# Relative attention: other written-out orders for four engines, and the second head's relative products among the first head's maxima

## What is computed

```python
B, S, D, NH, DK, MRP = 2, 2048, 256, 16, 16, 64        # 32 heads in all (2 x 16)
idx = clip(r[None, :] - r[:, None], -MRP, MRP) + MRP    # distance, cut at 64
logits = einsum('bhqd,bhkd->bhqk', q, k) + einsum('bhqd,qkd->bhqk', q, embK[idx])
w = softmax(logits)
out = einsum('bhqk,bhkd->bhqd', w, v) + einsum('bhqk,qkd->bhqd', w, embV[idx])
```

## Time and profile before

| | before |
|---|---|
| median of 3 runs | 4203.42 us (4187.34 to 4205.01) |
| the profiled execution | 4198.53 us; span 4196.8 us, granted clock 0.933 |
| PE busy | 3844.2 us (92%) |
| DVE busy | 3390.2 us (81%) |
| ACT busy | 2865.1 us (68%) |
| POOL busy | 1488.6 us (35%) |
| DMA | mean 151 GB/s; SP's queue 57.9% of 16 engines' span |

### The profile page before, as it was taken

The page is one execution under the profiler, slowest core; times in us unless marked ns, Lnnn a source line. Parts: engine busy times, 40 slices in busy tenths (PEclk is TensorE's granted clock), DMA queues, the critical chain, the costliest instruction groups (busy, mean ns, idle before and its releaser), DMA issues. The chain is left out here.

```text
span 4196.8 us, 76647 instructions
## 1 busy us (share of the span) xinstructions
PE 3844.2 (92%) x26302; PEld 2105.0 (50%) x26302; DVE 3390.2 (81%) x6328; ACT 2865.1 (68%) x5771; POOL 1488.6 (35%) x1457
## 2 busy tenths in 40 slices
PE   8599999999999999996879999999999999869998
PEld 5255555555555555553533333333333333659998
DVE  7688889898998888953779999999999992657776
ACT  4077778787877777883217777777777776236666
POOL 0356667666666666651000101000001000523333
PEclk9589999999999999998969999999999996779999
DMA  8667777777777777744763424343334320789997
GB/s 313 167 144 174 163 169 177 172 177 169 172 171 169 170 168 168 168 118 135 238 124 58 72 50 77 52 72 60 63 64 70 56 60 23 172 283 325 323 326 220
DMA packets 477915, 634.98 MB, mean 151 GB/s; under 512 B 60900, under 2 KB 403668, under 8 KB 463316
## 3 DMA queue, kind: packets, MB, share of 16 engines
q1 hardware_dynamic: 458996, 606.74, 57.9%
q0 software_dynamic: 18528, 23.34, 2.9%
HBM read 412.95 MB, written 215.89 MB: 150 GB/s over the span
## 5 line engine op out<-in xcount | busy, mean ns | idle before, releaser
L1140 ACT ACTIVATE ra_p<-ra_psS 128x512 f32<-128x512 f32 x2048 | 1112.6, 602 | 328.5 <-PE ra_psS L1211 242.5
L396 DVE TENSOR_REDUCE pa_pm<-pa_psA 128x2 f32<-128x1024 f32 x1024 | 1208.6, 1220 | 136.5 <-PE pa_psA L472 136.3
L444 ACT ACTIVATE pa_p<-pa_psS 128x512 f32<-128x512 f32 x2048 | 1064.3, 603 | 297.3 <-PE pa_psS L490 293.4
L1055 DVE TENSOR_REDUCE ra_pm<-ra_psA 128x1 f32<-128x896 f32 x1024 | 1113.2, 1087 | 167.7 <-PE ra_psA L1181 110.0
L490 PE MATMUL pa_psS<-pa_qs,pa_zs 50*128 50x512 f32 x2048 | 811.3, 475 | 67.5 <-ACT pa_p L444 37.6
L1181 PE MATMUL ra_psA<-ra_zs,ra_qs 48*128 48x512 f32 x2048 | 778.0, 466 | 76.0 <-DVE ra_pm L1057 51.2
L472 PE MATMUL pa_psA<-pa_zs,pa_qs 48*128 48x512 f32 x2048 | 802.4, 475 | 33.0 <-DMA pa_zs<-k_halves 18.3
L1211 PE MATMUL ra_psS<-ra_qs,ra_zs 50*128 50x512 f32 (+3 forms) x2176 | 725.7, 419 | 2.0 <-ACT ra_p L1140 1.9
L490 PEld LDWEIGHTS pa_psS<-pa_qs,pa_zs 50*128 50x128 f32 x2048 | 348.1, 188 | 636.3 <-ACT pa_p L444 599.5
L1244 PE MATMUL ra_psO<-ra_p,ra_vs 128*32 128x128 f32 (+2 forms) x6400 | 572.1, 464 | 0.0
L500 PE MATMUL pa_psO<-pa_p,pa_vs 128*32 128x512 f32 x4096 | 560.9, 621 | 0.0
(11 more groups left out here) (238 smaller groups left out, 4752.6 us busy)
## 6 DMA issues: line engine op xcount, KB each, us to landing
mo_w_parts<-second_weight_parts SPq DMA_DIRECT2D x39, 2048.0 KB, 9.3
relative_rows<-ra_rst SPq DMA_DIRECT2D x128, 512.0 KB, 5.5
ra_blk<-window_rows SPq DMA_DIRECT2D x128, 512.0 KB, 4.1
ra_zs<-k_halves SPq DMA_DIRECT2D x192, 248.0 KB, 7.8
mo_w_raw<-ffn_W SPq DMA_DIRECT2D x39, 1024.0 KB, 11.7
ra_dl<-relative_rows SPq DMA_DIRECT2D x128, 256.0 KB, 4.6
window_rows<-ra_pc SPq DMA_DIRECT2D x128, 256.0 KB, 4.9
pa_qs<-q_halves SPq DMA_DIRECT2D x192, 128.0 KB, 6.4
```

What stands on the lines that cost most here:

```text
L396: dve.reduce_max(pm[:, par, 2 * a:2 * a + 2], psA[w][:, :, :], AX.X).then_inc(s_am.h, 1)
L444: act.activation(pr[:, i % NPR, :], psS[:, slot(i), :], ACT.Exp).then_inc(s_ex.h, 1)
L1055: dve.reduce_max(pm[:, q, i, 2 * left:2 * left + 1], psA[w][:, lo:lo + 2 * G - P], AX.X).then_inc(s_far.h, 1)
L1140: act.activation(dst, psS[:, slot(t, i), :], ACT.Exp if kind == "E" else ACT.Copy).then_inc(s_cp.h, 1)
```

## The change

All engines get new orders for a body. PE's strings and the kinds of the ring are other permutations, of the same counts; the exps stand before other fills; REL_AHEAD is 18 instead of 19. Product 1 now comes after three units instead of two, product 2 after seven instead of behind unit 32, product 3 and M directly behind unit 32. On SP, the write and read of chunk 2 come before the loads for the head after next, the window read 2 stands ahead of the reads of chunks 1 and 2. On POOL, fold_p(t, 2) stands ahead of join_p(t, 3), part_r(t+2, 2) ahead of join_p(t+1, 0), lay_v behind fold_p(t, 1). In the opening, head 1's four products stand behind units 19, 22, 25 and 28 of head 0. SUM_TURNS is as it was.

```diff
@@ -543,12 +543,12 @@
 NROT = 15
 NZ = 2 * NROT + 1
 W = 2 * P
-REL_STEPS = ("sRO", "asasssaaRsssO", "saaassasaasO", "sasasaaO", "saasO", "saasassaO", "assaaasssasaO", "asssaRsO",
-             "saassRO", "asaassasO", "MsssaassaasasaO", "aassaasO", "asassasaO", "aassasaO", "asasssaassasaO",
-             "saasasaOsaas")
-RING_KINDS = "EEEEEEEEEEEEWEEEEEEWWEEEEEEEWEEEEWFEEEEEEEWEEEEEFWEWEFEEEEEEEEEEEEEF"
-WX_AT = (38, 41, 42, 45, 52, 55, 58, 72, 75, 85, 87, 89, 89, 90, 92, 95)
-REL_AHEAD, REL_LEAD = 19, 9
+REL_STEPS = ("RO", "saassasasssaassRsO", "saassaaO", "asassaassRsO", "saasO", "saaasasO", "ssaasaassasaO",
+             "aassasaO", "RssO", "MssaasO", "asassasassaasasaO", "asasasaO", "saasO", "aasssaaO",
+             "aassasasaasssaasO", "aassaasOasass")
+RING_KINDS = "EEEEEEEEEEEWEWWEWEEEEEEEWEEEEEEEEEEFEWEEEEEEFEEEEWEWEFEEEEEEEEEEEEFE"
+WX_AT = (43, 44, 52, 52, 54, 57, 59, 69, 73, 74, 74, 84, 89, 98, 100, 103)
+REL_AHEAD, REL_LEAD = 18, 9
 RC_REL = 7
 SUM_TURNS = ((1, 24), (0, 1), (0, 10), (0, 18))
 
@@ -591,6 +591,7 @@
 RING = ring()
 NR = len(RING)
 RTURNS = TURNS + 4
+R_BETWEEN = (19, 22, 25, 28)
 UN = 2
 LEFT, RIGHT, LEFT_FIRST, RIGHT_LAST = range(4)
 
@@ -638,8 +639,12 @@
 
     body = rel_turns()
     units = [n for n, (kind, _) in enumerate(body) if kind == "A"]
-    first = [("R", c) for c in range(4)] + [("A", a) for a in range(32)] + [("M", None)]
-    first += [("R", 4 + c) for c in range(4)] + [("A", 32 + a) for a in range(REL_AHEAD)]
+    first = [("R", c) for c in range(4)]
+    for a in range(32):
+        first.append(("A", a))
+        if a in R_BETWEEN:
+            first.append(("R", 4 + R_BETWEEN.index(a)))
+    first += [("M", None)] + [("A", 32 + a) for a in range(REL_AHEAD)]
     PT = len(first)
     NPR = 16
     place = {x: n for n, x in enumerate(RING)}
@@ -852,12 +857,14 @@
             for g in range(NG):
                 sp.dma_start(dr_p.rearrange("t (a i) q r -> (t a) i q r", a=4)[g].rearrange("i q r -> q i r"),
                              ptr[:, 0:NT // 4 * W].rearrange("p (i r) -> p i r", r=W)).then_inc(s_zd.h, 16)
+            write_r(1, 1, 0)
+            for c in range(3):
+                write_r(1, 1, c + 1)
+                read_r(1, 1, c)
             send_m(0, 0)
+            read_r(1, 1, 3)
             s_zd.wait(sp, 16 * NG)
             write_p(0, 0, 0)
-            for c in range(4):
-                write_r(1, 1, c)
-                read_r(1, 1, c)
             read_p(0, 0, 0)
             s_am.wait(sp, 32)
             load_stack(2, 0, 0, s_qa)
@@ -886,27 +893,27 @@
                     if divide:
                         store_reciprocals(n)
                     if third:
+                        write_r(t + 2, p, 2)
+                    read_p(t, p, 2)
+                    if third:
                         read_r(t + 2, p, 1)
-                    read_p(t, p, 2)
                     if divide:
                         spread_reciprocals(n)
+                    if third:
+                        read_r(t + 2, p, 2)
                     if t + 3 < HEADS:
                         s_am.wait(sp, 32 * (t + 2))
                         load_stack(t + 3, p + 1, 0, s_qa)
                     write_p(t, p, 3)
                     if third:
-                        write_r(t + 2, p, 2)
                         write_r(t + 2, p, 3)
-                    read_p(t, p, 3)
                     if more:
                         send_m(t + 1, p + 1)
-                    if third:
-                        read_r(t + 2, p, 2)
-                    if more:
-                        write_p(t + 1, p + 1, 0)
+                    read_p(t, p, 3)
                     if third:
                         read_r(t + 2, p, 3)
                     if more:
+                        write_p(t + 1, p + 1, 0)
                         read_p(t + 1, p + 1, 0)
                     if divide:
                         store_o(t, n)
@@ -1008,36 +1015,38 @@
             for c in range(4):
                 part_r(0, c)
             lay_v(0, 0, 1)
+            part_r(1, 0)
+            part_r(1, 1)
             join_p(0, 0, 0)
-            for c in range(4):
-                part_r(1, c)
+            part_r(1, 2)
+            part_r(1, 3)
             fold_p(0, 0)
             join_p(0, 0, 1)
             for it in range(HEADS // U):
                 for p in range(U):
                     t, n = U * it + p, 2 * it + p // 2 - 1
                     more, third = t + 1 < HEADS, t + 2 < HEADS
+                    join_p(t, p, 2)
+                    fold_p(t, 1)
                     if more:
                         lay_v(t + 1, p + 1, it + 1 + (p + 1) // U)
-                    join_p(t, p, 2)
-                    fold_p(t, 1)
                     if third:
                         part_r(t + 2, 0)
+                    fold_p(t, 2)
                     join_p(t, p, 3)
                     if third:
                         part_r(t + 2, 1)
-                    fold_p(t, 2)
+                        part_r(t + 2, 2)
                     if more:
                         join_p(t + 1, p + 1, 0)
                     fold_p(t, 3)
                     if p % 2 == 0 and n >= 0:
                         divide(n)
                     if third:
-                        part_r(t + 2, 2)
                         part_r(t + 2, 3)
                     if more:
+                        join_p(t + 1, p + 1, 1)
                         fold_p(t + 1, 0)
-                        join_p(t + 1, p + 1, 1)
 
         @blk.vector
         def _(dve):
```

## The result

| | before | after |
|---|---|---|
| median | 4204.22 us (4 runs, 4187.34 to 4222.74) | 4330.68 us (4 runs, 4318.05 to 4341.03) |
| ratio after / before | | 1.0304, 95% interval 1.0264 to 1.0345 |
| the profiled execution | 4198.53 us, clock 0.933 | 4341.03 us, clock 0.900 |
| bodies 1 to 29 | 1547.18 us, 53.35 each | 1690.56 us, 58.30 each |

The change costs 3.0%. The forecast was 4272 us with a range of 4140 to 4325: the direction was right, the size too small, and the result lies above the range. The profiled execution of after is the longest of its four, 10 us above the median, so the traces differ by 142.5 us where the medians differ by 126.5.

What follows compares the result with a forecast made beforehand. PE and DVE share the bound; SP's queue and the DMA decide how much is lost. Bodies lose 171.3 instead of 85.9 us (+85.4), less 11.7 of the opening: +73.7 on 4198.53, so 4272 us, range 4140 to 4325.

Steps and rivals of the forecast that it cites:

- opening: Ahead of body 0: head 1's products among head 0's maxima start head 1 earlier, saving 11.7 us (9 to 13).
- waits of DVE for POOL in bodies 1 to 29: Per body 3.0 us in 7 ordinary even, 3.5 in 15 odd, 6.1 in 7 with V.
- what a body loses beyond its wait: In each waiting body, a fee of 1.9 us for the halved clock.
- loss of before's bodies, taken off: Bodies 1 to 29 of before: 85.9 us above 29 undisturbed bodies of 50.39, replaced by the new 171.3.
- the new wait: At turn 18, DVE waits for join_p(3), held up by fold_p(2) and its late window read: 3.0 us in even bodies.
- rival A: Window read goes out early, so the new wait is only 0.9 to 1.4 us: 4154 or 4136 us; chance 0.27.
- The signs named: DVE waits some 3 us in nearly each body, fold waits for window_rows, bodies of 55 to 58 us, clock under 0.96.
- The old wait: At unit 32, DVE waits for masked relative rows, 45.6 us in 21 waits; to stay only in every fourth body.
- the fee: In bodies 1 to 29, what a wait costs on average besides itself: 1.9 us, from the halved clock.
- rival B: After turn 24, a second wait, for join_p(t+1, 0) behind two part_r: 2 us a body, 58 in all, 4330; chance 0.10.
- B's reason against itself: At the sum after turn 24: PE is late itself at half clock, said against the second wait of 2 us.

Runs made afterwards that it cites:

- e10: e8 with SP's load of V at the end of the body and POOL's lay_v behind fold_p(1): 4154.34 us, ratio 0.9894 to before.
- e12: e10 with SP's loads of the head after next moved behind the write and read of chunk 3: 4103.77 us, ratio 0.9813 to before.
- e7: The kernel before with the new opening alone, all bodies as they were: 4189.55 us against 4188.24, ratio 0.9978.
- e1: The kernel after with DVE's sum of chunk 3 after turn 22 instead of 18: 4385.1 us, ratio 1.0447 to before.
- e9: The kernel after with fill 46 computed 12 times over into the same bank: 4346.13 us, ratio 1.0349 to before.
- e5: The kernel after with POOL's whole body order of before: 4210.12 us, ratio 1.0057 to before.
- e4: The kernel before with POOL's fold_p(2) ahead of join_p(3), alone: 4228.47 us, ratio 1.0117.
- e3: The kernel after with POOL's fold_p(2) back behind join_p(3): 4290.65 us, ratio 1.0246 to before.
- e6: e5 with the exps of the next head's chunk 0 before fills 43 to 46: 4221.2 us, ratio 1.0071 to before.
- e11: The strings, exps and SP order of after on e10's POOL order, with chunk 0's exps as in e6: 4202.27 us, ratio 0.9992 to before.
- e8: e7 with SP's read of chunk 0's relative rows ahead of the next head's loads: 4163.76 us, ratio 0.9939 to before.

## Why the prediction was right, and where it was wrong

Its sum beside the two traces, in us:

| term | forecast | measured |
|---|---|---|
| opening | -11.7 | -5.9 by the end of body 0 |
| waits of DVE for POOL in bodies 1 to 29 | 116.2 | 115.7 |
| what a body loses beyond its wait | 29 x 1.9 = 55.1 | 1690.56 - 1461.3 - 115.7 = 113.6 |
| loss of before's bodies, taken off | -85.9 | -85.9 |
| after body 29 | 0 | +5.0 |
| together | +73.7 | +142.5 |

**Right: the new wait, its place, its cause and its size.** In ordinary even bodies DVE waited 3.3 us (forecast 3.0), in odd ones 3.4 and 3.1 (3.5), in V bodies 6.2 (6.1). The steps behind it stood in the same order, about 1 us earlier than said: window read issued at 20.8 (22.2), fold at 25.3 (26.2), keeps done at 29.8 (30.6), DVE due at 26.7 (27.6). The window read went out late, as said, and rival A fell: the write of body 12 was issued at 923.93 and the read at 932.48, 8.6 us later. That loads in front of a write can make such a delay is shown for chunk 3 (e10 and e12), not for this read by itself. The signs named were there, with bodies of 55.6 to 62.6 and a clock of 0.88. The old wait was left in the V bodies alone, as said.

The Trainium skill (DMA: Bandwidth & Descriptors, "Queues, rings and completion order") has each DMA engine consume the descriptors of a ring in order; the 9.5 and 4.5 us of e10 and e12 agree.

**Right in the first half: the opening.** The first maximum of head 1 came at 187.96 (forecast 186.2), the first relative product of body 0 at 214.05 instead of 225.48, 11.4 earlier. But body 0 then took 62.0 us instead of 56.4 and gave half of it back. In e7, with the old bodies, 7.5 us were left. The step that failed is that the earlier start of body 0 was booked as the gain, while the waits were summed over bodies 1 to 29 alone. In after, body 0 has the wait of the sum after turn 24 too (2.56 us) and 26.2 us at 1.2 GHz instead of 17.1; its tail takes 17.6 us instead of 15.0.

**Wrong: the price of what lies beyond the wait.** The failed step is the fee, (85.9 - 45.6) / 21 = 1.9 us per wait, and with it the rejection of rival B. Two things were missed: of the 58 us by which the forecast for the bodies was short, the first is 43 (head: 5.5 x 29 = 160 measured, 116.2 forecast) and the second 15 (tail: 70 measured, 55.1 forecast).

First, the deadline that ends last in a body was not the one priced. The sum gave the chain only as far as the right part of chunk 3 (30.6). Carried on from there with durations that stood in the trace of before, it is 1.4 for the sum of join_p(3), 2.7 and 2.7 for two part_r, 2.9 for keeps: 40.3, for a sum that stood at 35.4 in body 12 of before. The rows of before that give these lengths:

```profile
892.50 1.29 POOL L979 TENSOR_TENSOR ra_pc<-ra_pc,ra_tmp 128x512 f32<-128x512 f32 x1
893.86 1.29 POOL L944 TENSOR_TENSOR ra_dr<-ra_dl,masks 128x512 f32<-128x512 f32 x1
895.23 1.29 POOL L944 TENSOR_TENSOR ra_dl<-ra_dl,masks 128x512 f32<-128x512 f32 x1
...
898.21 1.55 POOL L944 TENSOR_TENSOR ra_pc<-ra_sw,masks 128x128 f32<-128x128 f32 x2
899.84 1.28 POOL L944 TENSOR_TENSOR ra_tmp<-ra_sw,masks 128x512 f32<-128x512 f32 x1
```

So the head would end 4.9 late, not 3.0: the 2 us of rival B. Measured were 39 to 41 in ordinary bodies of after, e1 and e9, at full clock or half, with a wait at turn 18 or without. B's reason against itself, that PE is late anyway at half clock, confused the sign with the price. The half clock did hide the second wait (no wait in the row at 951.29, 2.5 us in e9, 5.3 in e1). It didn't make it free: the head ended at the same time in all three. That both chains of after, POOL's and the exps behind PE at half clock, end within 0.6 us of each other is chance, and no run here has part_r(2) moved back by itself.

Second, the clock. In before the half clock lies wholly in the head (3.9 us a body, none in the tail) and ends before the sum after turn 24. In after it lasts until the tail, and the tail takes 17.4 us instead of 15.0, 2.4 x 29 = 70 us. A fee taken as constant per wait cannot show this: DVE's wait per waiting body grew from 2.2 to 4.0 us, PE's idle stretches of over 0.4 us from 29.0 to 105.7 us in all, and the time at 1.2 GHz from 116 to 416 us, in both kernels some 4 us of it for each us of PE's idleness (no constant either: in e5 it is 167 for 80.9, 2.1). Taken in proportion to the waits, (85.9 - 45.6) / 45.6 = 0.9 us per us, the same rows would have given 116.2 x 1.88 = 219 for the bodies and 4320 in all.

That B's figure, 4330, is the measured median is partly chance. Its place was right, and its sum for the bodies, 171.3 + 58 = 229.3 us, is what they lost (1690.56 - 1461.3). But two of its terms miss by some 15 us each and cancel: waits and chain 116.2 + 58 = 174 against 160 in the head (40.9 - 35.4 = 5.5 a body), the fee 55.1 against 70 in the tail.

**How the parts share the loss.** POOL's order carries 107 of 143 us (e5). Of its moves, the fold ahead of join_p(3) alone costs 46 us in the old kernel (e4), but taking it back in the new one returns only 23.5 (1690.56 against 1667.11 us in e3), where the sum after turn 24 still waits. POOL's rows put that wait behind part_r(2), which now stands ahead of join_p(t+1, 0). The rest, 36 us, goes with the strings, the ring, the exps and SP's order; PE's waits for the folds (e5, e6, e11) point at the place of the F banks and exps against POOL's folds, but these were not separated by a run.

## What to carry to other kernels

Follow a late engine's queue to its last deadline in the period, not to the first that it misses, and ask of each experiment whether a wait went or only moved. A period's end is the latest of several chains, so a stall that a slow stretch hides can still set it: here neither taking away the first wait (e1) nor the half clock of the head (e9) moved the head's end, and POOL's old order (e5) did. On SP's queue, put a short transfer that someone waits for in front of bulk loads: here three such steps (e8, e10, e12, the second with a move on POOL) took the bodies from 53.35 to 50.86 us.

## What was not expected of the hardware

- Half clock costs by its place. In the head, 9.7 us of it in after against 1.3 in e1 left the head's length as it was (40.9 and 40.3). In the tail, each us at 1.2 GHz cost 0.33 to 0.53 us over the 14.9 or 15.0 of the undisturbed tail (after 2.4 for 4.6, e9 3.1 for 8.0, e3 4.4 for 12.6, e1 4.8 for 14.4). The wait ahead of it did not add: the three tails of e9 at full clock behind an idle stretch of 2.2 us took 14.9.
- In body 12, idle stretches of PE of 2.2 us (e9) and 2.57 us (after) were followed by 10 us windows at a granted 0.50, though PE was busy for 9.90 and 10.00 us of them; in e9 it had been busy for 9.08 of the 10 us from 953.00, which take in the start of the idle stretch. The same 2.2 us cost other bodies of e9 anything from nothing to 20.5 us at 1.2 GHz.
- Redundant work kept the clock up: with fill 46 computed 12 times the clock stayed at 1.00 through a wait of 3.2 us, and the head was as long as in after (40.7 against 40.9).
- Waits of DVE of up to 1.7 us left the clock alone in e4, longer ones did not. This is no sharp rule: in before, body 5 ran 13.7 us at 1.2 GHz behind a wait of DVE for POOL of 1.0 us, with PE idle for 0.45 and 0.41 us.
